# A four-stage transformer block as one software pipeline: a third hand-written order for each engine, and 18 counter increments per round in TensorE's queue

## The chip, the cores and the metric

One Trainium2 chip, one of its cores. The core has five engines that run their own instruction queues and meet only at semaphores: TensorE (PE in the profile, its weight loads PEld), VectorE (DVE), ScalarE (ACT), GpSimd (POOL) and SyncE (SP, which only starts transfers here). The metric is the device time of one execution in microseconds, the median of several runs.

## The reference

The input `x` is 128 x 64 x 128 in float32, or 64 tiles of 128 rows by 128 features; the context has the same shape. Four blocks follow each other, and the first three add their result to `x` after a layer norm without gain or bias:

```python
x = x + attention0(layernorm(x), ctx)     # 16 heads of 8, with biases, softmax over a row of 64 context positions
x = x + experts(layernorm(x))             # 8 experts 128->128->128 with relu, weights from the top 2 of a gate
x = x + attention1(layernorm(x), ctx)     # 16 heads of 8, no biases
x = x + recurrent(layernorm(x))           # the recurrence below
# recurrent, over 128 time steps of 64 rows:
f = sigmoid(xt @ wf.T + c @ uf.T + bf)
i = sigmoid(xt @ wi.T + c @ ui.T + bi)
g = tanh(xt @ wc.T + c @ uc.T + bc)
c = f * c + i * g
h = tanh(x @ wo.T + c_final @ uo.T + bo)  # needs the last c, for every tile
```

Two facts set the shape of the work. Each of the first three blocks is local to a tile (a tile is two sequences of 64). The fourth carries the state `c` through all 128 half tiles in order, and the output of every tile needs the last state.

## The kernel before, in words

Everything stays on chip: `x` and the context are read once, in 11 chunks each, and the output is written once at the end. The work is cut into rounds. In round `i` each engine does its part of every stage, for tiles of different age: the stages of the first attention work on tile `i` less a lag, those of the experts 5 tiles behind (`L1`), the second attention 8 behind (`L2`), the recurrence 13 behind (`L3`). Rounds run from 0 to 79 (`FIRST`, `LAST`). Rounds 0 to 14 fill the pipeline, in rounds 15 to 62 every stage has a tile, after that the stages run dry one by one.

Within a round each engine's operations stand in an order written out by hand, as a list of `for r in due(i, name)` loops (for TensorE lines 547 to 628, for ScalarE 824 to 903, for VectorE 1118 to 1232, for GpSimd 1365 to 1408). `LAG` says how many rounds after its tile's number an operation comes; `AHEAD` moves an operation by whole rounds in one phase of the kernel, and `due` makes up for the move where phases meet (it runs an operation twice in a round or not at all). The kernel before has two orders per engine: one for rounds 0 to 62 and one for rounds 63 to 79 (`LATE = NT + -1`). In the second, most operations are moved back by a round, so that round 63 has little in it.

TensorE's operations, with the names that the text uses and the lines of the profile: `kv` keys and values of a tile (L308, L309, L317), `turnx` transposes of the normalized rows (L331), `q` queries (L346), `S` scores (L366), `e0` to `e3` transposes of the exponentials (L381), `rt` (L392), `pv` attention times values (L411), `p` output projection (L425), `gate` (L435), `h0` and `h1` first expert layer (L446), `turnw` (L456), `y0` and `y1` second expert layer (L467), `yb` expert bias (L479), `wx0` and `wx1` the output's input share (L492, L508), `xin` the recurrence's input share (L526), `sA` and `sB` the recurrence's two half steps (L539). In float32 each matmul of the code is two passes in the queue, each a weight load and a matmul; the transposes are one. `sA`, `sB`, `pv`, `S` and half of `kv` consist of many small passes on parts of the array, the others of whole ones.

The half step `sA` needs the state `C`. After it ScalarE takes three activations (`gA`, L815 to L817) and VectorE three operations (`uA`, L1093 to L1097), which make the next `C`; then `sB`, `gB`, `uB` likewise. `xin` of the next tile waits for the `C` of `uB` (line 524).

PSUM has eight banks. One holds the recurrence; the other seven are given out in turn to the results of TensorE's operations. `USES` lists the operations in TensorE's order with the reader that frees the bank, and each operation waits for that reader. Where an operation has several waits, the last one rides on its first pass and the others are instructions of their own in TensorE's queue, two waits each.

A full round of the kernel before has 236 passes, so 472 weight loads and matmuls, and 22 waits of their own: 494 instructions (495 where a chunk of the context begins).

Of the kernel before, what the change touches and what calls it, by code (L numbers as in the profile page):

```python
# [34 lines left out]
WARM = 4  # L35

# [10 lines left out]
LAG = {"pv": 5, "sA": 2, "y0": 3, "e3": 4, "q": 2, "yb": 3, "turnx": 1, "e0": 4, "p": 5, "wx0": 10, "y1": 3,  # L47
# [7 lines left out]
OFF = (0, L1, L2, L3)  # L55
LAST_STEP = NT + L3 - 1 + LAG["sB"] - -1
FIRST, LAST = 0, NT + 16

SPAN = {"C": (0, NT), "N": (0, NT + L3), "A": (0, NT + L2), "F": (L1, NT), "Z": (L3, NT),
        "W0": (LAST_STEP - 6 - LAG["wx0"], (NW + 1) // 2), "W1": (LAST_STEP - 6 - LAG["wx1"], NW // 2)}  # L60
# [4 lines left out]
USES = [("pv", "aT", 5, "A", 1, 1), ("y0", "acc", 3, "F", 8, 5), ("e3", "ET3", 4, "A", 1, 1),  # L65
# [7 lines left out]
USES_LAST = [("y0", "acc", 3, "F", 8, 5), ("y1", "xm", 3, "F", 1, 1), ("kv", "kvc", 1, "C", 1, 1),  # L73
# [7 lines left out]


FULL, LATE = FIRST, NT + -1
AHEAD = {"y0": (0, 0, -1), "q": (0, 0, -1), "turnx": (0, 0, -1), "e0": (0, 0, -1), "p": (0, 0, -1),
# [12 lines left out]


def phase(i):
    return 0 if i < FULL else 1 if i < LATE else 2  # L100
# [13 lines left out]
def build(nc, x_d, c_d, w_d, out):  # L114
    ctx = ExitStack()
    with ctx:
# [104 lines left out]
        for i in range(FIRST, LAST):  # L221
            for name, reader, lag, chain, step, first in (USES_LAST if i >= LATE else USES):
                made = 0
                for r in due(i, "S" if name[0] == "S" else name):
                    n = r - lag - SPAN[chain][0]
                    if name == "kv" and n <= 0:
# [6 lines left out]
                place += max(made, 1)  # L233
# [49 lines left out]
        def tensor_program(e):  # L283
            def bank(i, name, done=()):
# [6 lines left out]
                return banks[bank_at[name, j]]  # L291

# [144 lines left out]
            def hidden(i, c):  # L437
# [20 lines left out]
            def experts(i, c):  # L458
# [7 lines left out]
                for n in range(4):  # L466
                    m = e.matmul(b[:, 128 * n:128 * n + 128], hT[:, t % 2, 4 * c + n, :], w2[:, 4 * c + n, :],  # L467
                                 start=True, stop=True, skip_group_check=True)
                m.then_inc(sig(f"y{c}"), 1)
# [11 lines left out]
            def out_inputs(i, u):  # L481

                g = 2 * (i - LAST_STEP + 6) + u
# [12 lines left out]
            def inputs_share(m):  # L496

                lo = TAIL[MINE[m]][1]
                if m == 0:

                    for name, reader, _, chain, step, first in USES:
# [14 lines left out]
            def cell_inputs(i):  # L516
# [30 lines left out]
            for i in range(FIRST, LATE):  # L547
                if i == FIRST + 2:
                    project_bias()
                values(i)  # L550
                step(i, 0)
                for r in due(i, "y0"):
                    experts(r, 0)
                turn_e(i, 3)
                for r in due(i, "q"):
                    query(r)
                expert_bias(i)
                for r in due(i, "turnx"):
                    turn_x(r)
                for r in due(i, "e0"):  # L560
                    turn_e(r, 0)
                for r in due(i, "p"):
                    project(r)
                out_inputs(i, 0)
                for r in due(i, "y1"):
                    experts(r, 1)
                for r in due(i, "e2"):
                    turn_e(r, 2)
                for r in due(i, "e1"):
                    turn_e(r, 1)  # L570
                for r in due(i, "gate"):
                    gate(r)
                for r in due(i, "turnw"):
                    turn_w(r)
                for r in due(i, "rt"):
                    turn_r(r)
                for r in due(i, "h0"):
# [3 lines left out]
                out_inputs(i, 1)  # L581
# [8 lines left out]
            for i in range(LATE, LAST):  # L590
                for r in due(i, "y0"):
                    experts(r, 0)
                for r in due(i, "y1"):
                    experts(r, 1)
                for r in due(i, "kv"):
                    keys_values(r)
                out_inputs(i, 0)
                for r in due(i, "sB"):
                    step(r, 1)
                for r in due(i, "turnx"):  # L600
                    turn_x(r)
                for r in due(i, "p"):
                    project(r)
                for r in due(i, "e1"):
                    turn_e(r, 1)
                for r in due(i, "turnw"):
                    turn_w(r)
                out_inputs(i, 1)
                for r in due(i, "q"):
                    query(r)  # L610
                for r in due(i, "e0"):
                    turn_e(r, 0)
                for r in due(i, "gate"):
                    gate(r)
                for r in due(i, "e2"):
                    turn_e(r, 2)
                for r in due(i, "h0"):
                    hidden(r, 0)
                turn_e(i, 3)
                for r in due(i, "S"):  # L620
                    scores(r)
                for r in due(i, "h1"):
                    hidden(r, 1)
                for r in due(i, "xin"):
                    cell_inputs(r)
                expert_bias(i)
                step(i, 0)
# [880 lines left out]
```

## Time and profile before

| | us |
|---|---|
| three timed runs | 846.52, 847.08, 849.42 (median 847.08) |
| profiled execution, span from the first to the last instruction | 848.5 |
| busy in it: PE / PEld / DVE / ACT / POOL | 822.1 / 739.4 / 769.7 / 783.1 / 686.1 |

The profiled execution was not timed separately; its span lies within the three times, 1.4 us above their median. Busy time counts how long an engine has something in hand. For TensorE it is modelled from pipelined passes, so a busy PE need not be a full one: how far apart the same operation starts in successive rounds tells more. Waits and semaphore increments are instructions of the queue, but are not counted as busy and stand in no row.

### The profile page before, as it was taken

Reading aid. Unit: us, or ns where it says so; the run is one execution under the profiler, and the core shown is the slowest. Engines: PE = TensorE matmul, PEld = TensorE weight load, DVE = VectorE, ACT = ScalarE, POOL = GpSimd, SP = SyncE. Lnnn points to the kernel's source line nnn. Section 1 sums busy time; section 2 is a strip of 40 time slices with the busy share of each in tenths; the row PEclk is TensorE's granted clock in tenths of the full one; section 3 lists DMA queues with packets and bytes.
Section 4 is the critical chain, followed back from the end, with each engine's and each line's share of the span. In section 5 each row is a group of like instructions: output and inputs, shape, how many; then the busy total and the mean of one; then the engine's idle time right before and its main releaser. Section 6 shows DMA issues by size and latency. Waiting matters only on the chain. (4 is left out here: it accounts for less than half of the span.)

```text
span 848.5 us, 41475 instructions
## 1 busy us (share of the span) xinstructions
PE 822.1 (97%) x15268; PEld 739.4 (87%) x15268; DVE 769.7 (91%) x2778; ACT 783.1 (92%) x2490; POOL 686.1 (81%) x1292
## 2 busy tenths in 40 slices
PE   7899999999999999999999999999999999999996
PEld 4688898999999999999999899999998988888784
DVE  5689999999999999999999999999999998999755
ACT  4899999999999999999999999999999999988864
POOL 4788998888888888888888888888888887877634
PEclk7899999999999999999999999999999999999999
DMA  9400000000000000000000000000000000000005
GB/s 348 166 2 3 2 3 4 3 3 4 3 4 3 3 3 3 4 3 4 3 3 3 3 4 3 3 4 3 3 3 3 4 3 3 3 4 3 3 3 199
DMA packets 6965, 17.67 MB, mean 21 GB/s; under 512 B 752, under 2 KB 2288, under 8 KB 6768
## 3 DMA queue, kind: packets, MB, share of 16 engines
q1 hardware_dynamic: 6336, 14.36, 4.4%
q8 instruction: 125, 2.05, 1.0%
q10 hardware_dynamic: 432, 0.68, 0.2%
q14 instruction: 72, 0.59, 0.2%
HBM read 10.84 MB, written 4.19 MB: 18 GB/s over the span
## 5 line engine op out<-in xcount | busy, mean ns | idle before, releaser
L976 DVE TENSOR_REDUCE mx<-ps 128x8 f32<-128x512 f32 (+1 forms) x288 | 166.8, 621 | 11.9 <-PE ps L366 11.8
L1305 POOL TENSOR_TENSOR h<-Ex 128x512 f32<-128x512 f32 (+1 forms) x144 | 166.0, 1153 | 10.7 <-ACT Ex L734 8.1
L990 DVE TENSOR_TENSOR Ex<-ps,mx 128x512 f32<-128x512 f32 (+1 forms) x288 | 167.4, 622 | 0.0
L745 ACT ACTIVATE ET<-ps 128x512 f32<-128x512 f32 (+1 forms) x288 | 155.3, 573 | 11.1 <-PE ps L381 8.9
L734 ACT ACTIVATE Ex<-Ex 128x512 f32<-128x512 f32 (+1 forms) x288 | 163.8, 596 | 0.0
L1082 DVE SCALAR_TENSOR_TENSOR acc<-ps,we,acc 128x128 f32<-128x128 f32 x448 | 150.9, 337 | 11.9 <-PE ps L467 0.5
L783 ACT ACTIVATE hT<-ps,w 128x128 f32<-128x128 f32 x512 | 149.0, 400 | 4.7 <-PE ps L446 4.6
L381 PE MATMUL ps<-w,Ex 128*128 128x128 f32 x1024 | 149.8, 275 | 1.5 <-ACT qT L722 0.7
L446 PEld LDWEIGHTS ps<-xT,w 128*128 128x128 f32 x1024 | 124.1, 191 | 24.8 <-issue 24.6
L446 PE MATMUL ps<-xT,w 128*128 128x128 f32 x1024 | 142.2, 282 | 0.0
L467 PE MATMUL ps<-w,hT 128*128 128x128 f32 x1024 | 139.5, 281 | 0.3 <-DVE Ex L990 0.3
L467 PEld LDWEIGHTS ps<-w,hT 128*128 128x128 f32 x1024 | 123.7, 192 | 5.5 <-DVE Ex L990 0.5
L381 PEld LDWEIGHTS ps<-w,Ex 128*128 128x128 f32 x1024 | 119.4, 142 | 4.3 <-ACT qT L722 1.8
L1289 POOL TENSOR_TENSOR rs<-ve,half 128x4 f32<-128x4 f32 (+3 forms) x77 | 71.6, 929 | 59.5 <-DVE ve L966 59.5
L707 ACT ACTIVATE xn<-x,mr,rs 128x128 f32<-128x128 f32 x256 | 109.7, 540 | 6.1 <-POOL mr L1291 6.1
L1309 POOL TENSOR_TENSOR h<-h 128x256 f32<-128x256 f32 (+1 forms) x144 | 97.6, 678 | 20.7 <-POOL h L1305 0.4
L366 PE MATMUL ps<-Km,qT 32*64 32x256 f32 x2048 | 75.1, 394 | 4.0 <-ACT xT L691 1.1
L539 PE MATMUL ps<-CG,w 128*32 128x64 f32 x3072 | 70.3, 222 | 3.0 <-issue 2.2
L1262 POOL TENSOR_TENSOR Km<-kT,w 128x512 f32<-128x512 f32 x64 | 66.6, 1041 | 6.0 <-ACT kT L662 5.8
L411 PE MATMUL ps<-ET,Vb 128*32 128x64 f32 x4096 | 71.2, 220 | 0.0
L1262 POOL TENSOR_TENSOR Km<-kv,w 128x512 f32<-128x512 f32 x64 | 66.7, 1042 | 0.2 <-issue 0.2
L411 PEld LDWEIGHTS ps<-ET,Vb 128*32 128x32 f32 x4096 | 65.9, 110 | 0.4
(108 smaller groups left out, 1793.7 us busy)
## 6 DMA issues: line engine op xcount, KB each, us to landing
cx<-ctx_dram SPq DMA_DIRECT2D x7, 512.0 KB, 12.3
x<-x_dram SPq DMA_DIRECT2D x7, 512.0 KB, 14.1
out_dram<-x SPq DMA_DIRECT2D x14, 256.0 KB, 2.7
w<-weights_dram SPq DMA_DIRECT2D x2, 512.0 KB, 5.8
w<-weights_dram SPq DMA_DIRECT2D x1, 576.0 KB, 8.5
out_dram<-x SPq DMA_DIRECT2D x4, 128.0 KB, 2.6
w<-weights_dram ACTq DMA_DIRECT2D x1, 328.0 KB, 5.2
w<-weights_dram ACTq DMA_DIRECT2D x1, 256.0 KB, 3.1
```

Source lines behind the costliest of these rows:

```text
L381: m = e.transpose(b[:, 128 * n:128 * n + 128], Ex[:, j % 2, r, 128 * n:128 * n + 128], ident)
L411: m = e.matmul(b[32 * r:32 * r + 32, 128 * c + 64 * n:128 * c + 64 * n + 64], Vb[:, c, j % 4, n, r, 2 * w:2 * w + 2, :].rearrange("p a c - ...
L446: m = e.matmul(b[:, 128 * n:128 * n + 128], w1[:, 4 * c + n, :], xT[:, (t + L1) % 2, 1, :], start=True, stop=True, skip_group_check=True)
L467: m = e.matmul(b[:, 128 * n:128 * n + 128], hT[:, t % 2, 4 * c + n, :], w2[:, 4 * c + n, :], start=True, stop=True, skip_group_check=True)
L734: e.activation(Er, Er, ACT.Exp, scale=SCALE).then_inc(sig(f"E{r}"), 1)
L745: e.activation(ET[:, j % 2, r, lo:hi, :, :], b[:, 256 * lo:256 * hi].rearrange("p (c w q) -> p c w q", c=hi - lo, w=2), ACT.Copy).then_inc ...
L783: m = e.activation(hT[:, t % 2, k, :], b[:, 128 * n:128 * n + 128], ACT.Relu, bias=col[:, B1 + k:B1 + k + 1])
L976: e.tensor_reduce(mx[:, j % 2, r, 4 * lo:4 * hi], b[:, 256 * lo:256 * hi].rearrange("p (j k) -> p j k", k=64), AX.X, ALU.max).then_inc(sig ...
L990: e.tensor_tensor(Ex[:, j % 2, r, 256 * lo:256 * hi].rearrange("p (j k) -> p j k", k=64), b[:, 256 * lo:256 * hi].rearrange("p (j k) -> p ...
L1082: m = e.scalar_tensor_tensor(x[:, t, :] if n == 8 else d, b[:, 128 * k:128 * k + 128], we[:, t % 2, n - 1:n], d, ALU.mult, ALU.add)
L1262: e.tensor_tensor(Km[:, j % 2, c, :, :], k.unsqueeze(1).to_broadcast([P, 4, 128]), hmask.unsqueeze(2).to_broadcast([P, 4, 128]), ALU.mult) ...
L1305: e.tensor_tensor(u, v[:, :, :, 0:32], v[:, :, :, 32:64], ALU.add).then_inc(sig("half1"), 1)
```

## The change

Three things. First, each engine has three orders: for rounds 0 to 14, 15 to 71 and 72 to 79. All three are new; `LAG`, `AHEAD` and the bank plan `USES` are rewritten to fit (one plan per phase). Second, six places of TensorE's program call `filler(1)`, which puts an instruction into the queue that computes nothing and raises a semaphore `fill` that nobody waits for: after each of the four matmuls of `h0`, `h1`, `y0`, `y1` and after two of the three of `xin`, 18 in a round, from tile 2 on. Third, the loops are written so that every operation goes through `due`. No arithmetic, no transfer and no semaphore between engines is added or taken away.

```diff
+EVEN = 2
+STARTS = (0, 15, 72)
+FIRST, LAST = STARTS[0], 80
+OUT = NT + 9
 def phase(i):
-    return 0 if i < FULL else 1 if i < LATE else 2
+    return max(sum(i >= s for s in STARTS) - 1, 0)
...
+            def filler(n):
+                for _ in range(n):
+                    e.nop(nofuse=True).then_inc(sig("fill"), 1)
...  (in hidden and experts)
                 for n in range(4):
                     m = e.matmul(b[:, 128 * n:128 * n + 128], w1[:, 4 * c + n, :], xT[:, (t + L1) % 2, 1, :],
                                  start=True, stop=True, skip_group_check=True)
+                    filler(t >= EVEN)
...  (in cell_inputs, of three)
+                    filler(t >= EVEN and n < 2)
```

TensorE's orders, in the names of above:

```
before, rounds 0-62:  pv sA y0 e3 q yb turnx e0 p wx0 y1 e2 e1 gate turnw rt h0 sB wx1 S h1 xin kv
before, rounds 63-79: y0 y1 kv wx0 sB turnx p e1 turnw wx1 q e0 gate e2 h0 e3 S h1 xin yb sA pv rt
after, rounds 0-14:   pv y0 e3 q yb turnx p e0 wx0 y1 e2 gate e1 turnw rt sA h0 wx1 S h1 xin sB kv
after, rounds 15-71:  sA pv yb y0 e3 wx0 turnx e1 p e0 wx1 y1 e2 gate q rt turnw h0 sB S h1 xin kv
after, rounds 72-79:  turnw gate h0 e1 p turnx y1 y0 wx1 e0 q kv e2 h1 e3 xin S sA pv rt wx0 sB yb
```

VectorE's in the full rounds (`mx`, `sb` maxima and differences of the scores, `c0` to `c8` the experts' sums, `st`, `ag` the layer norms' statistics):

```
before: sb1 mx2 mx3 sb2 sb3 aT sm c0 st0 c1 rc c2 xa c3 c4 c5 uA c6 gsc c7 c8 st13 st2 gtop ag uB gidx mx0 mx1 sb0
after:  st2 st13 ag uB mx1 mx0 mx2 sb1 gidx sb0 sb2 aT c0 sm mx3 c1 sb3 c2 rc c3 xa c4 uA c5 st0 c6 gsc c7 c8 gtop
```

ScalarE and GpSimd are reordered in the same way, with `gA` behind the first exponential and `gB` before the last one on ScalarE. A full round of TensorE's queue now has 494 + 18 = 512 instructions (513 in six of the full rounds, where a chunk begins).

## Rows read from the trace of the kernel before

**Rows 1.** The page's first part: span, busy time and count of each engine.

```profile
span 848.5 us, 41475 instructions
PE 822.1 (97%) x15268; PEld 739.4 (87%) x15268; DVE 769.7 (91%) x2778; ACT 783.1 (92%) x2490; POOL 686.1 (81%) x1292
```

**Rows 2.** Busy time by stretch: from:to, length, busy (instructions) by engine, PEclk, DMA.

```profile
14.90:27.00 12.10, 10.89 (x89) 6.83 (x93) 7.16 (x27) 7.38 (x25) 8.21 (x15) 0.50 1.03 408
...
38.70:117.30 78.60, 74.30 (x1141) 65.94 (x1137) 71.66 (x260) 72.65 (x235) 68.42 (x143) 1.00 0.01 3
117.30:684.80 567.50, 565.26 (x11100) 521.92 (x11096) 543.17 (x1927) 554.06 (x1741) 485.90 (x894) 1.00 0.01 3
684.80:829.90 145.10, 140.13 (x2653) 123.39 (x2644) 119.22 (x475) 123.43 (x422) 100.72 (x207) 1.00 0.01 3
```

**Rows 3.** TensorE in order of time: start, length, line, passes [idle before <-releaser].

```profile
117.33 1.08 PE L411 MATMUL ps<-ET,Vb 128*32 128x64 f32 x64
...
322.49 1.08 PE L411 MATMUL ps<-ET,Vb 128*32 128x64 f32 x64
...
323.83 1.16 PE L467 MATMUL ps<-w,hT 128*128 128x128 f32 x8
...
329.29 1.06 PE L446 MATMUL ps<-xT,w 128*128 128x128 f32 x8
...
330.75 1.12 PE L366 MATMUL ps<-Km,qT 32*64 32x256 f32 x32
...
334.46 1.08 PE L411 MATMUL ps<-ET,Vb 128*32 128x64 f32 x64
335.36 0.52 PE L539 MATMUL ps<-CG,w 128*32 128x64 f32 x24
...
684.85 1.08 PE L411 MATMUL ps<-ET,Vb 128*32 128x64 f32 x64
```

**Rows 4.** TensorE in order of time, where the half step is cut in two.

```profile
130.19 0.39 PE L539 MATMUL ps<-CG,w 128*32 128x64 f32 x10
130.99 0.42 PE L539 MATMUL ps<-CG,w 128*32 128x64 f32 x14 [0.41 <-issue]
...
467.16 0.28 PE L539 MATMUL ps<-CG,w 128*32 128x64 f32 x4
467.94 0.53 PE L539 MATMUL ps<-CG,w 128*32 128x64 f32 x20 [0.50 <-issue]
...
480.00 0.39 PE L539 MATMUL ps<-CG,w 128*32 128x64 f32 x13
480.70 0.41 PE L539 MATMUL ps<-CG,w 128*32 128x64 f32 x11 [0.31 <-issue]
```

**Rows 5.** The view of waits: who waited for what, us in total, times, longest.

```profile
PE ps L539 <- issue: 2.2, 6, 0.5
```

**Rows 6.** The DMA queues: packets, MB, share of 16 engines.

```profile
q8 instruction: 125, 2.05, 1.0%
```

**Rows 7.** The page's fifth part: the shortest weight loads of TensorE.

```profile
L411 PEld LDWEIGHTS ps<-ET,Vb 128*32 128x32 f32 x4096 | 65.9, 110 | 0.4
```

**Rows 8.** The recurrence in a full round, all engines in order of time.

```profile
331.30 0.32 ACT L817 ACTIVATE CG<-ps,w 128x64 f32<-128x64 f32 x1
...
332.14 0.23 DVE L1097 SCALAR_TENSOR_TENSOR CG<-ps,ig 128x64 f32<-128x64 f32 x1
...
332.79 0.83 PE L526 MATMUL ps<-cx,w 128*128 128x128 f32 x6
```

**Rows 9.** TensorE in order of time, at the change of orders and at the end.

```profile
698.33 0.23 PE L479 MATMUL ps<-b2s,weT 72*128 72x128 bf16 x1 [0.74 <-ACT kv L672]
...
825.71 0.54 PE L539 MATMUL ps<-CG,w 128*32 128x64 f32 x24 [0.41 <-DVE CG L1097]
...
827.84 0.91 PE L526 MATMUL ps<-cx,w 128*128 128x128 f32 x6 [0.43 <-DVE CG L1097]
```

More of the change, by code:

```diff
@@ L221, in build @@
         for i in range(FIRST, LAST):
-            for name, reader, lag, chain, step, first in (USES_LAST if i >= LATE else USES):
+            for name, reader, lag, chain, step, first in USES[phase(i)]:
                 made = 0
@@ L232, in build @@
                         made += 1
-                place += max(made, 1)
+                place += max(made, i >= 0)
         def bank_of(name, j):
@@ L499, in inputs_share @@
                 if m == 0:
-                    for name, reader, _, chain, step, first in USES:
+                    for name, reader, _, chain, step, first in USES[0]:
                         if name != "turnx":
@@ L576, in tensor_program @@
                     turn_r(r)
+                for r in due(i, "sA"):
+                    step(r, 0)
+                for r in due(i, "h0"):
+                    hidden(r, 0)
+                for r in due(i, "wx1"):
+                    out_inputs(r, 1)
+                for r in due(i, "S"):
+                    scores(r)
+                for r in due(i, "h1"):
+                    hidden(r, 1)
+                for r in due(i, "xin"):
+                    cell_inputs(r)
+                for r in due(i, "sB"):
+                    step(r, 1)
+                for r in due(i, "kv"):
+                    keys_values(r)
+            for i in range(STARTS[1], STARTS[2]):
+                for r in due(i, "sA"):
+                    step(r, 0)
+                for r in due(i, "pv"):
+                    values(r)
+                for r in due(i, "yb"):
+                    expert_bias(r)
+                for r in due(i, "y0"):
+                    experts(r, 0)
+                for r in due(i, "e3"):
+                    turn_e(r, 3)
+                for r in due(i, "wx0"):
+                    out_inputs(r, 0)
+                for r in due(i, "turnx"):
+                    turn_x(r)
+                for r in due(i, "e1"):
+                    turn_e(r, 1)
+                for r in due(i, "p"):
+                    project(r)
+                for r in due(i, "e0"):
+                    turn_e(r, 0)
+                for r in due(i, "wx1"):
+                    out_inputs(r, 1)
+                for r in due(i, "y1"):
+                    experts(r, 1)
+                for r in due(i, "e2"):
+                    turn_e(r, 2)
+                for r in due(i, "gate"):
+                    gate(r)
+                for r in due(i, "q"):
+                    query(r)
+                for r in due(i, "rt"):
+                    turn_r(r)
+                for r in due(i, "turnw"):
+                    turn_w(r)
                 for r in due(i, "h0"):
@@ L589, in tensor_program @@
                     keys_values(r)
-            for i in range(LATE, LAST):
+            for i in range(STARTS[2], LAST):
+                for r in due(i, "turnw"):
+                    turn_w(r)
+                for r in due(i, "gate"):
+                    gate(r)
+                for r in due(i, "h0"):
+                    hidden(r, 0)
+                for r in due(i, "e1"):
+                    turn_e(r, 1)
+                for r in due(i, "p"):
+                    project(r)
+                for r in due(i, "turnx"):
+                    turn_x(r)
+                for r in due(i, "y1"):
+                    experts(r, 1)
@@ new lines, in tensor_program @@
+                for r in due(i, "h1"):
+                    hidden(r, 1)
+                for r in due(i, "e3"):
+                    turn_e(r, 3)
+                for r in due(i, "xin"):
+                    cell_inputs(r)
+                for r in due(i, "S"):
+                    scores(r)
+                for r in due(i, "sA"):
+                    step(r, 0)
+                for r in due(i, "pv"):
+                    values(r)
+                for r in due(i, "rt"):
+                    turn_r(r)
@@ L598, in tensor_program @@
+                for r in due(i, "wx0"):
+                    out_inputs(r, 0)
                 for r in due(i, "sB"):
                     step(r, 1)
[L600 to L625, printed above, removed]
@@ L626, in tensor_program @@
-                expert_bias(i)
-                step(i, 0)
-                values(i)
-                for r in due(i, "rt"):
-                    turn_r(r)
+                for r in due(i, "yb"):
+                    expert_bias(r)
             for n in (5, 6):
@@ L823, in scalar_program @@
             e.activation(identb[:, :], ident, ACT.Copy).then_inc(sig("identb"), 1)
-            for i in range(FIRST, LATE):
-                if i == FIRST + 8:
+            for i in range(FIRST, STARTS[1]):
+                if i == 8:
                     e.wait_ge(sig("in_w6"), 16)
@@ new lines, in scalar_program @@
+            for i in range(STARTS[2], LAST):
+                for r in due(i, "re1"):
+                    relus(r, 1)
+                for r in due(i, "sc"):
+                    scale(r)
+                for r in due(i, "xo0"):
+                    out_inputs(r, 0)
+                for r in due(i, "gB"):
+                    gates(r, 1)
+                for r in due(i, "ET1"):
+                    turn_e(r, 1)
+                for r in due(i, "xT"):
+                    turn_x(r)
+                for r in due(i, "ex3"):
+                    exps(r, 3)
+                for r in due(i, "ex1"):
+                    exps(r, 1)
+                for r in due(i, "xo1"):
+                    out_inputs(r, 1)
+                for r in due(i, "ET0"):
+                    turn_e(r, 0)
+                for r in due(i, "re0"):
+                    relus(r, 0)
+                for r in due(i, "qc"):
+                    query(r)
+                for r in due(i, "ET2"):
+                    turn_e(r, 2)
+                for r in due(i, "wd"):
+                    widen(r)
+                for r in due(i, "ET3"):
+                    turn_e(r, 3)
+                for r in due(i, "ex0"):
+                    exps(r, 0)
+                for r in due(i, "gA"):
+                    gates(r, 0)
+                for r in due(i, "weT"):
+                    turn_w(r)
@@ L1117, in vector_program @@
             e.memset(acc[:, :, :], 0.0).then_inc(sig("zeros"), 1)
-            for i in range(FIRST, LATE):
-                if i == FIRST + 3:
+            for i in range(FIRST, STARTS[1]):
+                if i == 3:
                     e.wait_ge(sig("bvo"), 1)
@@ L1159, in vector_program @@
                     combine(r, 8)
+                for r in due(i, "gtop"):
+                    gate_top(r)
+            for i in range(STARTS[2], LAST):
+                for r in due(i, "xa"):
+                    project(r)
+                for r in due(i, "uB"):
+                    update(r, 1)
+                for r in due(i, "sm"):
+                    sums(r)
                 for r in due(i, "st13"):
                     stats_attention(r)
+                for r in due(i, "c2"):
+                    combine(r, 2)
@@ L1199, in vector_program @@
+                for r in due(i, "uA"):
+                    update(r, 0)
+                for r in due(i, "c1"):
+                    combine(r, 1)
                 for r in due(i, "c8"):
```

445 lines of the change are left out of this document (275 added, 170 removed), and 73 rows, old and new, of tables (AHEAD, LAG, USES, USES_LAST).

## The prediction, made before the changed kernel ran

> **What bounds the kernel now.** I read the page's busy times first, then the busy times by stretch, then TensorE in order of time, and last the waits and the DMA queues. TensorE is busy for 97% of the span, the others for 81 to 92% [rows 1], but a share says little where every engine is near its limit. The stretches cut the run into a fill up to 117.3 us, full rounds up to 684.8, a drain up to 829.9, and 18.6 us at the end in which the last state becomes the output [rows 2]. The full rounds are two thirds of the time. There TensorE has 565.26 us of 567.50 in hand, ScalarE 554.06, VectorE 543.17 [rows 2]: TensorE is the bound, and ScalarE is only 2.4% behind it.
>
> The reader should then take one operation and see how far apart it starts. `pv` starts at 322.49 and at 334.46, 11.97 us apart (11.975 over several such rounds) [rows 3], and in such a round no gap stands between TensorE's groups. 47 rounds lie between the `pv` of 117.33 and that of 684.85: 567.52 us, or 12.07 a round [rows 3]. At 11.975 each they would take 562.8. So 4.7 us were lost in the full rounds, though not evenly.
>
> The loss has one face. Six times the half step on L539 is cut in two, and TensorE is idle before its second part with "issue" as the reason, which means that nothing of another engine held it [rows 5]. In the second of these rows the first part starts at 467.16 with 4 passes and the rest follows at 467.94; four passes of this kind take under 0.1 us, so the cut costs some 0.7 us [rows 4]. The cuts come in pairs, in successive rounds, and the place moves: after 4 passes and then after 13 [rows 4]; the pair at 130 us moves from 10 to 19, the one at 636 us, whose rows look the same, from 1 to 10. Nine passes are 18 instructions. A round has 494 instructions, so a place that moves on by 18 per round is a place that comes every 512 instructions of the queue. Queue 8 brought TensorE's instructions in 125 packets [rows 6]; 30,536 weight loads and matmuls [rows 1] and some 1,560 waits, counted in the program, over 125 make 257 for a packet. Two packets are 512. So the cuts sit at the edge between two blocks of instructions, of 256 each. Numbering the queue's instructions, all six lie before number 197 of a block as the program counts it.
>
> Not every edge costs. Edges pass through the whole round, about one position in 27 rounds, and only those that fall into the half step behind `pv` cut. The reason must be that the block just left was short: from the scores (330.75), where the edge before it lies, to the half step (335.36) is 4.6 us for 256 instructions [rows 3], against 6 on average, and the passes there are so small that TensorE has no work in hand to cover a late block.
>
> **The change, part by part.** *The 18 increments, what they fix.* The edges are pinned. I counted the new queue, round by round, from the orders and the waits; the same count gives the old queue's 494s and places. From round 16 on the two edges of a round lie at positions 48 and 304 of 512, and drift to 42 and 298 by round 64 because of six rounds of 513. The first is where `sA` ends and `pv` begins, the second where `h0` begins. In the clean round from the end of the half step (323.83) to `h0` (329.29) are 5.46 us [rows 3]; `pv`, now behind the half step, adds 0.89 (from 322.49 to the half step behind it). So the blocks take 6.35 and 11.98 - 6.35 = 5.63 us: neither is near 4.6. In the old kernel the edges stood in the same part of the work in rounds 24, 38 and 53, and `pv` came 11.98 us apart there. The holes go: -4.7 us.
>
> *What they cost.* No row shows such an instruction. Below, zero, since they stand between whole matmuls of 0.11 us a pass, four instructions to 0.22 us, which is time in which the queue runs ahead; less than zero is excluded, as they only add. Above, if nothing covered them and each cost what the shortest weight load takes, 110 ns [rows 7], 18 x 0.11 = 1.98 us a round and 123 us over 62 tiles. I take zero: the 22 waits of a round are likewise instructions of their own, 16 of them directly before such groups, and the groups follow without idle time. The cover is gone where TensorE's queue has run empty, which in full rounds it does only at the cuts.
>
> The Trainium skill has a rule that speaks against the whole idea: the page "Runtime: NRT & Kernel Launch", section "Instruction fetch mechanics", says that the engine fetches the next block of 256 instructions by itself and that crossing a boundary is "mostly hidden". The spacing of the cuts agrees with its 256, but the six cuts are not hidden. By that rule the cuts would have another cause and would stay, and the sum would be 4.7 us higher. The page "PSUM — Partial Sum Buffer", section "Engine vs sequencer instructions", says that a nop with an increment waits only until earlier instructions are handed over, not until they complete; no run here shows it yet, and it would price the increments at nothing.
>
> *The middle order, rounds 15 to 71.* TensorE does the same passes. The kinds of neighbours that cost a longer step (whole passes to small ones and back) come as often as before, so I give the round 11.98 us again; the bounds are -0.1, if the odd gap around `yb` closes, and what a new wait would bring, below. It also replaces the old second order in rounds 63 to 71. At the change of orders before, TensorE is idle for 0.74 us in round 63 [rows 9]. Now a change comes at round 15, where all stages begin to be full, and one at 72, where little is left. I charge 1 us for round 15, by the one at 63 and a little for what follows it.
>
> *The first order, rounds 0 to 14.* Up to 27 us the DMA engines are full (share 1.03, the clock at 0.50 of its full rate) [rows 2] and no order brings the data sooner: 0. From 38.7 to 117.3 TensorE is idle for 4.3 us, ScalarE for 5.95 and VectorE for 6.9 [rows 2]. An order that fits can win at most ScalarE's 5.95, since its work stays the same, and a bad one could lose as much. I take -2, a third.
>
> *The last rounds.* From 684.8 to 829.9 TensorE is idle for 5.0 us [rows 2], part of it waits of 0.4 us for the state [rows 9], which no order removes: half steps are serial. I take -3 of a possible -5, with the other end at +3.
>
> *The rest.* The output part after 829.9 is the same, as are transfers and their order on SP: 0.
>
> Sum, on the profiled execution: 848.5 - 4.7 + 0 + 1 - 2 - 3 = 839.8. The span is 1.4 us above the median of the runs, so the time comes to 838.4 us.
>
> **The rivals.** *A: the sum holds*, 838.4, with 833 to 843 for its own range. *B: the cuts go, the ends give nothing* or lose a little: 847.1 - 4.7 + 1 = 843.4, up to 847. For it: all three engines are above 91% busy in the fill already; against it: both old orders were also used for rounds that they do not fit. *C: a new wait in every full round*, my case on the slower side. Its place is the recurrence: in a clean round ScalarE ends `gB` at 331.62, VectorE makes `C` by 332.37, and `xin` starts at 332.79 [rows 8], with 0.4 us to spare. VectorE now does `uB` behind both statistics and the aggregation, and ScalarE has some 0.28 us free in a round. If the chain comes 0.25 us too late in 50 rounds, 12.5 us are added: 851. It decides from 0.17 us a round, where it eats the 8.7 us gained. Against it: `uB` stood behind the same three before, and `S` and `h1` (2 us) still lie between `sB` and `xin`. *D: the edges are pinned where they hurt.* My count could be off by some instructions at the start. If each of 50 rounds had a cut of 0.7 us: 838.4 + 35 = 873. The nearest bad place is 85 instructions behind the first edge in the old order, so the miscount would have to be large. *E: the increments aren't covered*: 838.4 + 123 = 961 at the upper bound. *F: the cuts are something else and stay*, the page's rule above: as a mechanism, the half step would be cut once the queue has been drained by `pv`, whatever the block. 838.4 + 4.7 = 843.1. Against it, the step of exactly 9 passes in all three pairs.
>
> **How the numbers follow.** A 0.57, B 0.16, C 0.13, D 0.05, E 0.03, F 0.06. I call a change of under 0.3%, or 2.5 us (844.5 to 849.6), no change. Faster: A, F and half of B, 0.71. Same: the rest of B and the mild part of C, 0.11. Slower: most of C, D and E, 0.18. The predicted time is A's, 838.4. The range takes in A, B, F and C up to its price: 832 to 851.
>
> **What would show it.** Cuts on L539 with "issue" gone, and `pv` at 11.98 us in every round from 16 to 64: the pinned edges are right. A cut in the same place of each round: D. More than 1.0 us from the start of `h0` or `y1` to what follows its 8 passes: E. A wait of `xin` for `C` or of TensorE for ScalarE in each round: C. If the first `pv` of round 15 does not come before 117 us and the drain after round 65 is not shorter, the orders for the ends gave nothing. The prediction is wrong if the full round is not 11.98 us.

## The result, and the profile after

The changed kernel takes 841.29 us (841.05 to 841.61, four runs), the kernel before took 847.14 on the same chip: ratio 0.9923, 95% interval 0.9904 to 0.9942. The forecast was 838.4, with 832 to 851 as its range. The profiled execution lasted 839.2 us against 848.5, so on the profiles the gain is 9.3 us, in the timed runs 5.9. That difference has a cause. In every run of which both are known, the time is 1.75 to 2.1 us above the span of the same execution (841.05 and 839.2 for this profile). So the profile of before, at 848.5, is of an execution of some 850.3 us, 3 us slower than the median; where most of that lay is told below.

The page of the kernel after, its first part, beside [rows 1]:

```profile
span 839.2 us, 42592 instructions
PE 820.6 (98%) x15268; PEld 743.5 (89%) x15268; DVE 775.3 (92%) x2778; ACT 775.4 (92%) x2490; POOL 682.5 (81%) x1292
```

TensorE makes the same 15,268 passes; the page counts 1,117 instructions more, of which 1,116 are the increments (18 for 62 tiles). Queue 8 brings 129 packets, where [rows 6] had 125. The busy times by stretch (from:to, length, busy with instructions, PEclk, DMA), cut at the first pass of round 7, 15, 62, 72 and 79, beside [rows 2]:

```profile
34.90:111.70 76.80, 74.72 (x1145) 65.96 (x1141) 71.48 (x259) 72.01 (x234) 68.09 (x143) 1.00 0.01 3
111.70:680.60 568.90, 568.90 (x11103) 527.02 (x11094) 547.17 (x1926) 547.78 (x1741) 483.69 (x896) 1.00 0.01 3
680.60:784.50 103.90, 102.61 (x1953) 93.78 (x1944) 98.53 (x380) 95.06 (x322) 81.75 (x169) 1.00 0.01 3
784.50:821.90 37.40, 35.33 (x728) 30.94 (x725) 22.26 (x102) 27.78 (x100) 17.20 (x34) 1.00 0.01 3
```

The same view of the kernel before, for the stretches from round 62 and from round 72, which it enters at 684.85 and 785.41:

```profile
684.80:785.40 100.60, 99.30 (x1879) 88.27 (x1870) 92.03 (x352) 91.28 (x304) 80.96 (x168) 1.00 0.01 3
785.40:829.20 43.80, 40.13 (x770) 34.42 (x769) 27.19 (x123) 31.53 (x116) 19.75 (x40) 1.00 0.01 3
```

Look at the second line of after. TensorE is busy for all of 568.90 us, without a hole, and yet the 47 rounds take 1.4 us *longer* than the 567.50 of before with its six cuts [rows 2]. The cuts are gone, and every round has become longer: 12.096 us where none is disturbed, against 11.977. TensorE in order of time shows it (start, length, line, passes):

```profile
305.83 1.10 PE L423 MATMUL ps<-ET,Vb 128*32 128x64 f32 x64
...
311.40 0.29 PE L447 MATMUL ps<-w,xT 128*128 128x8 f32 x2
311.55 0.69 PE L358 MATMUL ps<-xT,w 128*128 128x128 f32 x4
312.07 0.38 PE L404 MATMUL ps<-w,rd 128*128 128x128 f32 x2
312.29 0.22 PE L469 MATMUL ps<-identb,wep 128*72 128x128 bf16 x1
312.35 1.11 PE L458 MATMUL ps<-xT,w 128*128 128x128 f32 x8
313.39 0.54 PE L554 MATMUL ps<-CG,w 128*32 128x64 f32 x24
...
317.93 1.10 PE L423 MATMUL ps<-ET,Vb 128*32 128x64 f32 x64
```

`pv` (now L423) starts at 305.83 and at 317.93, 12.10 us apart; in [rows 3] it was 11.97. The places that grew are here: `q` (L358) takes 0.52 us until the next group starts, behind the gate's 8 columns (L447), where the old order gave it 0.446; and `h0` (L458) takes 1.04 us behind the single pass of `turnw` (L469), where it took 0.986 behind `rt`. These two make 0.08 + 0.05 us, and `rt` and `turnw` between them give 0.01 back: 0.12 us a round. The same groups of before, for comparison:

```profile
325.26 0.61 PE L346 MATMUL ps<-xT,w 128*128 128x128 f32 x4
325.71 0.22 PE L479 MATMUL ps<-b2s,weT 72*128 72x128 bf16 x1
...
329.00 0.23 PE L456 MATMUL ps<-identb,wep 128*72 128x128 bf16 x1
329.06 0.39 PE L392 MATMUL ps<-w,rd 128*128 128x128 f32 x2
329.29 1.06 PE L446 MATMUL ps<-xT,w 128*128 128x128 f32 x8
330.28 0.54 PE L539 MATMUL ps<-CG,w 128*32 128x64 f32 x24
```

`h1`, `y1` and `xin`, which carry increments too, start as far from what follows them as before (0.995, 0.894 and 0.670 us).

### The profile page after: what moved, and what is told of

It reads as the page before. It is cut to its first block, busy times and chain, and to the rows that moved or that the text cites. A ratio compares the mean times of both kernels' runs of the same rounds, so it can differ in the third digit from the quotient of the medians.

```text
span 839.2 us, 42592 instructions
## 1 busy us (share of the span) xinstructions
PE 820.6 (98%) x15268; PEld 743.5 (89%) x15268; DVE 775.3 (92%) x2778; ACT 775.4 (92%) x2490; POOL 682.5 (81%) x1292
## 4 chain that ended last, share of the span: by engine, by line
PE 90%; DVE 4%; ACT 3%; issue 2%; POOL 1%; DVEq 0%; POOLq 0%; ACTq 0%
PE ps L458 15%; PE ps L480 13%; PE ps L393 13%; PE ps L378 8%; PE ps L423 7%; PE ps L554 6%; PE ps L540 5%; PE ps L329 4%; PE ps L358 4%; PE ps L437 3%; PE ps L343 3%; PE ps L320 2%; PE ps L404 2%; PE ps L321 2%; PE ps L493 1%
## 5 line engine op out<-in xcount | busy, mean ns | idle before, releaser
L1120 DVE TENSOR_TENSOR Ex<-ps,mx 128x512 f32<-128x512 f32 (+1 forms) x288 | 170.8, 617 | 0.1
L819 ACT ACTIVATE ET<-ps 128x512 f32<-128x512 f32 (+1 forms) x288 | 166.0, 584 | 3.2 <-PE ps L393 2.9
L393 PE MATMUL ps<-w,Ex 128*128 128x128 f32 x1024 | 158.8, 275 | 0.1
L1212 DVE SCALAR_TENSOR_TENSOR acc<-ps,we,acc 128x128 f32<-128x128 f32 x448 | 147.9, 330 | 1.3 <-issue 0.2
L458 PEld LDWEIGHTS ps<-xT,w 128*128 128x128 f32 x1024 | 124.2, 191 | 24.6 <-issue 24.6
L458 PE MATMUL ps<-xT,w 128*128 128x128 f32 x1024 | 144.9, 284 | 0.0
L857 ACT ACTIVATE hT<-ps,w 128x128 f32<-128x128 f32 x512 | 140.1, 398 | 3.1 <-PE ps L458 2.8
L393 PEld LDWEIGHTS ps<-w,Ex 128*128 128x128 f32 x1024 | 121.4, 143 | 1.7 <-ACT qT L796 0.5
L423 PE MATMUL ps<-ET,Vb 128*32 128x64 f32 x4096 | 71.9, 220 | 0.0
L554 PE MATMUL ps<-CG,w 128*32 128x64 f32 x3072 | 68.2, 221 | 0.8 <-DVE CG L1227 0.8
L889 ACT ACTIVATE ps<-ps,w 128x64 f32<-128x64 f32 x128 | 36.8, 288 | 34.2 <-PE ps L554 33.8
```

The lines of the kernel that those rows point to most:

```text
L393: m = e.transpose(b[:, 128 * n:128 * n + 128], Ex[:, j % 2, r, 128 * n:128 * n + 128], ident)
L819: e.activation(ET[:, j % 2, r, lo:hi, :, :], b[:, 256 * lo:256 * hi].rearrange("p (c w q) -> p c w q", c=hi - lo, w=2), ACT.Copy).then_inc ...
L857: m = e.activation(hT[:, t % 2, k, :], b[:, 128 * n:128 * n + 128], ACT.Relu, bias=col[:, B1 + k:B1 + k + 1])
L1120: e.tensor_tensor(Ex[:, j % 2, r, 256 * lo:256 * hi].rearrange("p (j k) -> p j k", k=64), b[:, 256 * lo:256 * hi].rearrange("p (j k) -> p ...
L1212: m = e.scalar_tensor_tensor(x[:, t, :] if n == 8 else d, b[:, 128 * k:128 * k + 128], we[:, t % 2, n - 1:n], d, ALU.mult, ALU.add)
```

## The experiments

**One part at a time.** Four kernels ran beside each other: the changed kernel without the increments, the old orders with them, the increments begun later so that the edges move, and the new middle order with two pairs of operations put back.

```diff
 e1:                 for _ in range(n):
-                    e.nop(nofuse=True).then_inc(sig("fill"), 1)
+                    pass
```

> The changed kernel with its three orders, but filler() puts nothing into TensorE's queue, so that a full round has 494 instructions again. Theory (the 0.12 us by which the full round grew comes from the new order, and the cuts come from block edges that drift through the round): a round without a cut stays at 12.10 us, and cuts of 0.4 to 0.9 us come back in pairs of rounds, some 4 to 5 us in all, each pair 18 instructions apart: 845 to 846.5 us. Rival (the increments cost 0.12 us a round): the uncut round falls to 11.98 us, which over 50 rounds gives back 6 us, and with the cuts the time is 839 to 841 us. Rival (new orders alone avoid cuts): 841 us and no cuts.

Measured: 841.97 us, ratio to before 0.9938 (0.9921 to 0.9954), as the kernel after within the error. The undisturbed round is 12.086 us against 12.096 with increments, so they cost at most 0.01 us of it and not the 0.12. The theory was right on the round and missed the time (845 to 846.5 us), and the rival held by which the new orders alone avoid cuts: they hardly return. Four rounds are 0.05 to 0.13 us longer than a clean one, two others 0.03, no more. With the new orders the increments have little left to do.

```diff
 e2 (before, with the filler calls of the change):
+EVEN = 2
+                    filler(t >= EVEN)      # in hidden and experts
+                    filler(t >= EVEN and n < 2)   # in cell_inputs
```

> The kernel before with its own orders and only the 18 increments per round added; by the count of the queue its edges then lie 47 instructions into pv and at the start of h0 in all full rounds. Theory: full rounds of 11.98 us and no cut, so the 4.7 us of the cuts are saved and nothing else: 842.4 us, with 841.5 to 843.5. Rival (the increments cost 0.12 us a round): rounds of 12.10 us, 847 to 848 us. Rival (block edges are not the cause of the cuts): the cuts stay in six rounds and the time is 847 us.

Measured: 845.24 us, ratio 0.9974 (0.9959 to 0.999), a gain of 2.2 us (0.8 to 3.5) in the timed runs, less than the 4.7 that I had expected. No group of small passes is cut any more, and the stretch from round 15 to 62 takes 563.58 us where before took 567.52:

```profile
115.40:678.90 563.50, 563.50 (x11100) 520.96 (x11092) 542.12 (x1927) 553.91 (x1741) 485.75 (x894) 1.00 0.01 3
```

So in the old orders 18 increments bring 3.9 us in these rounds of the profile, and leave rounds of 11.98 us. The six cuts of before had lengthened their rounds by 4.0 us (0.70, 0.70, 0.86, 0.60, 0.65 and 0.49); the other 0.6 of the 4.7 lay in six rounds that were 0.06 to 0.17 longer without a listed cut, and e2 has ten such rounds of 0.03 to 0.09. The trace records each increment as a semaphore event of 51 ns, about 0.15 us apart between whole passes, and about 1 us ahead of the passes in hand. By the Trainium skill, page "PSUM — Partial Sum Buffer", section "Engine vs sequencer instructions", such an increment waits for no pass to complete; the trace agrees, with that 1 us.

```diff
-EVEN = 2
+EVEN = 8      # e3: the changed kernel
```

> The changed kernel with EVEN = 8 instead of 2: the increments begin six tiles later, 108 instructions fewer, so that the edges lie about 103 instructions into pv and 38 into the scores in every full round, where in the kernel before the edges of the cut rounds lay (counted from the start of the small passes). Theory: a cut of 0.4 to 0.9 us near the end of pv in each of some 49 rounds, full rounds of 12.5 to 13.0 us, 861 to 885 us. Rival (the cuts need something else than the place of the edge, such as the old order of pv and sA): no cuts, 841 us.

Measured: 841.66 us, ratio 0.9927 (0.9911 to 0.9944), no cut, where the theory had 861 to 885 us. My theory, that the edges only had to lie in a bad place, failed in the new order.

```diff
 e4 (TensorE, rounds 15 to 71, and its bank plan):
-gate, q, rt, turnw, h0
+q, gate, turnw, rt, h0
```

> The changed kernel; in rounds 15 to 71 TensorE's order is q, gate, turnw, rt, h0 instead of gate, q, rt, turnw, h0 (bank plan to fit), which are the neighbours that these operations had before. In the trace q after gate takes 0.08 us longer than q after e3, and h0 after turnw 0.05 us longer than h0 after rt. Theory (the step after a pass of 8 columns or of bf16 costs this): full round of 11.97 to 11.98 us, 50 to 57 rounds x 0.12 = 6 to 7 us less, 834.5 to 836 us. Rival (the bound is a chain through another engine): the idle time moves and the round stays at 12.10 us, 841 us.

Measured: 835.71 us, ratio 0.9858 (0.9842 to 0.9875): 5.6 us better than the changed kernel (5.5 by the two ratios). TensorE in order of time, the same stretch of a round:

```profile
322.50 0.61 PE L358 MATMUL ps<-xT,w 128*128 128x128 f32 x4
322.94 0.29 PE L447 MATMUL ps<-w,xT 128*128 128x8 f32 x2
323.08 0.23 PE L469 MATMUL ps<-identb,wep 128*72 128x128 bf16 x1
323.15 0.39 PE L404 MATMUL ps<-w,rd 128*128 128x128 f32 x2
323.37 1.06 PE L458 MATMUL ps<-xT,w 128*128 128x128 f32 x8
```

`q` takes 0.44 us until the next group, `h0` 0.98 (until 312.38 from 311.40 in the round before), the round 11.97. Eight of the 47 rounds are 0.15 to 0.17 us longer, 1.3 us in all; the extra lies between `sA` and `pv`, at the pinned edge, as in the three rounds of 12.25 us of the changed kernel. From round 15 to 62 it takes 564.04 us, 4.9 less than after:

```profile
112.40:676.50 564.10, 564.08 (x11104) 521.55 (x11100) 547.41 (x1926) 549.02 (x1741) 485.31 (x896) 1.00 0.01 3
```

TensorE is busy for all of this stretch too. Its busy time can't tell the two orders apart, the distance between starts does.

**Does the place of an edge matter at all?** e3 had said no for the new order. In the old one the question was open.

```diff
-EVEN = 2
+EVEN = 8      # e5: otherwise e2
```

> The kernel before, with its own orders, and 18 increments per round that start with round 8 of the hidden steps instead of round 2. Every full round then has 512 instructions, and by my count of the queue its two edges lie 19 to 20 instructions into the half step sA (L539 of before) and 37 to 38 into the scores S, in each of some 48 rounds. In the kernel before, six of the rounds whose edge lay near there had a cut of 0.42 to 0.72 us in sA.
> Theory (in the old order the place of the edge decides): a cut of 0.4 to 0.9 us in most of the 48 rounds, rounds of 12.4 to 12.9 us instead of 11.98, in all 865 to 885 us.
> Rival (a cut needs more than the place: a fetch of code that comes late for another reason): no cut or a few, rounds of 11.98, about 845 us, as with the increments from round 2 on (845.2).

Measured: 865.59 us, ratio 1.0198 (1.0181 to 1.0215). The theory held: 34 of the 47 rounds from 15 to 61 are longer than 12.12 us, by 20.0 us together. The time is at the low end of the 865 to 885 expected. The waits of this kernel (who waited for what, us in total, times, longest), where [rows 5] had 2.2 us:

```profile
PEld ps L548 <- issue: 17.1, 39, 0.8
PE ps L548 <- issue: 10.8, 28, 0.6
```

And two of its cuts in order of time, both after 11 passes, where the count had put the edge after 10:

```profile
263.79 0.39 PE L548 MATMUL ps<-CG,w 128*32 128x64 f32 x11
264.45 0.42 PE L548 MATMUL ps<-CG,w 128*32 128x64 f32 x13 [0.27 <-issue]
...
276.33 0.39 PE L548 MATMUL ps<-CG,w 128*32 128x64 f32 x11
277.25 0.42 PE L548 MATMUL ps<-CG,w 128*32 128x64 f32 x13 [0.53 <-issue]
```

```diff
 e6: e5, and TensorE, rounds 0 to 62:
-                values(i)
-                step(i, 0)
+                step(i, 0)
+                values(i)
```

> The kernel of e5 (old orders, edges pinned 19 to 20 into sA and 37 to 38 into S), with one thing changed: on TensorE the half step sA comes before the values pv in rounds 0 to 62, as in none of the other orders of before. The pair of passes of sA that were cut then stands next to others and the queue's own wait for the gates ends elsewhere.
> Theory (what made the kernel after nearly immune is which pass waits ahead of the edge: pv behind sA instead of sA behind pv): no cut or a few, rounds of 11.98 to 12.0, 843 to 846 us, even if e5 has cuts in most rounds.
> Rival (the immunity lies in the rest of the new order, or the place alone decides): cuts as in e5, the same time as e5 within 3 us. If e5 has no cuts, this run says only what the swap costs by itself: -0.5 to +0.5 us over the whole time.

Measured: 862.38 us, ratio 1.0165 (1.0147 to 1.0183). 22 rounds are longer than a clean one by 0.3 us or more, 16.0 us together, and the cut has moved with the edge, into `pv`:

```profile
433.64 0.94 PE L417 MATMUL ps<-ET,Vb 128*32 128x64 f32 x50
435.14 0.42 PE L417 MATMUL ps<-ET,Vb 128*32 128x64 f32 x14 [0.56 <-issue]
```

So it is not the half step that is cut but whatever lies at the edge, and the order of these two alone is not what protects the changed kernel. e6 has its edges where e3 has them (some 104 instructions into `pv`, 38 into `S`) and the same operations from `S` to `pv`; e3 has no cut.

The traces let one check the count itself. Number TensorE's records in order of time, two for each pass and one for each wait or increment, from the first in the profile. Before, e5, e6, e7 and e11 then have 60 pauses of more than 0.35 us between two weight loads of one group in rounds 15 to 62 (6, 28, 21, 4 and 1), and in all 60 the first load behind the pause has number 193 or 194 of its 256. The number of such edges in each trace is also that of queue 8's packets, 125 without increments and 129 with them. So the cuts lie at the edges, whatever passes stand there.

**What is late in a cut.** The trace has the start of each packet of queue 8. In e3, without cuts, the packet behind the edge in `S` starts 0.6 to 2.3 us after the weight load at that edge (median 1.4); in the cut rounds of before, e5 and e6 it starts 2.3 to 3.1 us after it. The next edge comes 4.4 to 4.6 us after the first, and TensorE goes on 2.2 to 2.9 us after the packet's start, in all 57 cuts of these three kernels that stop the weight loads for more than 0.35 us from one to the next. Nowhere in the full rounds of the twelve traces is a block entered less than 2.2 us after its packet has started. Late packet and early edge together make the cut.

Part of why the packet is late can be read from the increments, which TensorE's queue records as it comes to them. Those of one group are 0.15 us apart. In e6, behind the edge in `S`, one step is 0.3 us instead, and the packet starts 0.2 to 1.2 us after it, mostly 0.7. Between 125 and 680 us, in 19 of the 21 uncut rounds the long step ends 0.4 to 1.0 us after the edge, in 19 of the 20 cut rounds 1.8 to 2.0 us after it. So the lateness shows in TensorE's own queue before the packet starts; no packet of the other instruction queue goes with the cuts regularly. That this step is the request for the packet is my reading and not shown, and what puts it at the one or the other moment, and why seldom late in the new orders, stays open. The Trainium skill, page "Runtime: NRT & Kernel Launch", section "Instruction fetch mechanics", calls the crossing of a block "mostly hidden": e2, e3 and the changed kernel agree with it, 34 rounds of e5 don't.

**Are the increments still worth anything?**

```diff
 e7: e4, and
-                    e.nop(nofuse=True).then_inc(sig("fill"), 1)
+                    pass
```

> The kernel of e4 (the changed kernel with TensorE's middle order mended: q, gate, turnw, rt, h0) without the 18 increments, so 494 instructions a round and edges that drift through the round.
> Theory (the new orders alone avoid the cuts, as in e1, where three rounds were 0.04 to 0.13 us longer than a clean one; the increments are now worth 0.7 us at most): rounds of 11.97 us, 835.5 to 836.5 us against 835.7 with increments.
> Rival (with q and gate in the mended places the cuts come back when the edges drift, as in the kernel before): six or so cuts of 0.4 to 0.8 us, 838 to 841 us.

Measured: 836.54 us, ratio 0.9848 (0.9832 to 0.9865). The time can't be told from e4's. On the profile round 15 to 62 takes 565.09 us, 1.05 more than e4: four rounds are 0.4 to 0.6 us longer, each with a pause at an edge in `pv`. So a drifting edge can still be cut in the mended order, where e1 had no such round. The increments are worth about 1 us on this profile, and nothing that the timed runs show.

```diff
 e8 (the changed kernel, TensorE, rounds 15 to 71):
-gate, q, rt, turnw, h0
+gate, q, turnw, rt, h0
```

> The kernel after, with turnw and rt of TensorE's middle order swapped back (gate, q, turnw, rt, h0): h0 stands behind rt as in the kernel before, q still behind the 8 columns of the gate.
> Theory (two exposures make the longer round: q behind gate 0.08 us, h0 behind turnw 0.05 us, and they add up): the clean round is 12.04 to 12.05 us, between 11.97 of the mended order and 12.095 of the changed kernel, and the time about 838.5 us (837.5 to 839.5).
> Rival 1 (q alone makes all of it): 12.10 us, 841 to 842 us. Rival 2 (h0 alone, or the two only together): 11.97 us, about 835.7 us.

Measured: 839.26 us, ratio 0.9889 (0.9872 to 0.9905). The clean round is 12.05 us. The two exposures add up: 11.97, 12.05, 12.095.

**What protects the new order, and what the first order brings.**

```diff
-EVEN = 2
+EVEN = 8      # e11: otherwise e4
```

> The kernel of e4 (middle order mended: q, gate, turnw, rt, h0) with the increments from hidden step 8 instead of 2, so that the edges lie some 103 instructions into pv and 38 into S, as in e3, where there was no cut in any round. In e5 and e6 edges at the same places gave cuts in about 37 and 25 of 48 rounds, so what protects the changed kernel is not the place and not the order of sA and pv alone.
> Theory (the protection lies in the new order as a whole, in the stretch between pv and S or in the other engines' orders, and not in q standing behind the gate): no cut or a few, rounds of 11.97, 835.5 to 837.5 us.
> Rival (q behind the gate and rt ahead of turnw is what protects; e7 with the mended order had one cut of 0.3 us and more in pv, e1 had none): cuts of 0.2 to 0.9 us in half of the rounds, 845 to 855 us.

Measured: 835.32 us, ratio 0.9864 (0.9848 to 0.9881), one cut (at 150 us, in `pv`) and all other rounds from 16 to 61 at 11.97 or 11.98. The theory held: `q` behind the gate and `rt` ahead of `turnw` are not the protection. The remaining candidates are the rest of the stretch from `pv` to `S` and the orders of the other engines; they were not tried one by one.

```diff
-STARTS = (0, 15, 72)
+STARTS = (0, 11, 72)      # e12: otherwise e4
```

> The kernel of e4 with the middle order from round 11 on instead of from round 15, on every engine; the first order is left for rounds 0 to 10. From the first pass of round 11 to that of round 15 the kernel before took 43.80 us, the changed one 42.68 and e4 42.73.
> Theory (what the fill gained between rounds 7 and 15, 1.85 us in ten profiles alike, comes from an order that fits the filling rounds): the middle order, made for full rounds, gives it back in part, so this stretch takes 43.2 to 44.5 us, and the time is 836.2 to 837.5 us against 835.7.
> Rival (any of the new orders does as well as the first; the gain came from the lags or from the early rounds): 42.5 to 43.0 us, 835.5 to 836 us.

Measured: 838.2 us, ratio 0.9899 (0.9882 to 0.9915), 2.5 us more than e4 and 2.9 more than e11, which ran on the same chip; 836.2 to 837.5 us had been expected. The stretch from round 11 to 15, e4 first, then e12:

```profile
69.70:112.40 42.70, 41.84 (x662) 37.66 (x656) 41.76 (x137) 40.25 (x121) 38.56 (x74) 1.00 0.01 3
```

```profile
71.00:115.70 44.70, 41.11 (x665) 37.59 (x657) 42.21 (x138) 40.45 (x122) 40.01 (x76) 1.00 0.01 3
```

TensorE is idle for 3.6 us instead of 0.9. The middle order doesn't fit the rounds that fill; the loss is just above what I had given it (44.72 us from start to start, against 43.2 to 44.5).

The best kernels are e4, e7 and e11, at ratios of 0.9858, 0.9848 and 0.9864, which beat both originals and can't be told from each other.

## Why the forecast was right, step by step

The time fell into the range and the direction was right, but that it came this close is luck: errors of opposite sign met in the sum. The prediction's own last line, that it is wrong if the full round is not 11.98 us, went against it: the round is 12.096. Round starts of the two profiles give each term.

*The cuts, -4.7.* Right in the main. The six are gone; they were 4.0 of it. The mechanism was right for the old orders: e2 removes them by pinning alone, e5 brings them into 34 rounds by pinning badly. It is not needed for the new ones (e1, e3). The reason given, that the block just left was short, is half of it: e3 passes the same stretch in 4.4 us and is not cut, and the packet must also be late.

*The increments, 0.* Right: e2 keeps 11.98 us, e1 gains 0.01 a round. Rival E is out, though the sign that was to show it, more than 1.0 us from the start of `h0` to what follows, came: `h0` takes 1.04 us with and without increments (e1), so the sign could not tell E from a new neighbour.

*The middle order, 0.* This is the step that failed. "The kinds of neighbours that cost a longer step come as often as before" looked at whole passes beside small ones, and not at whole passes behind a pass of 8 columns or a single bf16 pass. The round is 12.096 us, 47 x 0.12 = +5.6 us, and three rounds of 12.25 add 0.45. e4 and e8 show both places and that they add up. Why a group takes longer behind a short pass no run shows.

*The hand-over at round 15, +1.* It costs nothing: rounds 15 and 16 take 12.09 us each.

*The first order.* For rounds 7 to 14 I took -2; it is 78.62 to 76.76 us, -1.9, and the profiles of e2, e5 and e6 (78.5 to 78.7) and of e1, e3, e4, e7 and e8 (76.7 to 76.9) repeat it. e12 bears out for rounds 11 to 14 that the order matters: they take 43.80 us in the old order, 42.68 to 42.74 in the new first one and 44.72 in the middle one. Ahead of round 7 I took 0, "the DMA engines are full"; the profile says -3.8 (38.71 to 34.90). Most of that is a slow execution of before. e2, e5 and e6 have the same instructions as before up to there and reach round 7 at 36.66, 36.46 and 35.23; the seven other kernels with the new first order, at 35.0 to 37.0. What differs is when the clock is low. These are busy times by stretch, whose third number from the right is the granted clock; first the kernel before:

```profile
20.00:24.00 4.00, 3.38 (x20) 2.20 (x27) 2.07 (x10) 3.82 (x15) 2.81 (x5) 0.50 1.04 412
24.00:28.00 4.00, 4.00 (x68) 2.79 (x68) 2.74 (x8) 1.65 (x6) 1.99 (x5) 0.50 1.03 408
```

Then e6, whose queues are the same up to this time:

```profile
20.00:24.00 4.00, 3.09 (x52) 1.98 (x54) 1.88 (x10) 3.34 (x13) 2.81 (x7) 1.00 1.03 408
24.00:28.00 4.00, 3.15 (x58) 2.25 (x58) 3.64 (x15) 3.82 (x15) 3.02 (x6) 1.00 1.03 406
```

With DMA just as full, one ran at 1.2 GHz and was busy for all 4.00 us, the other at 2.4 and had time to spare. So in that execution of before TensorE at its lower clock had become the limit at the end of the loading, and the DMA share of 1.03 in [rows 2] hid it. Both sets of kernels show either level between 10 and 28 us, at different moments. The starts of round 7 follow the moment at which the clock rises and then stays up until the output: in the eight kernels with the new first order it is 20.5, 20.8, 21.1, 21.4, 25.4, 26.5, 26.8 and 27.3 us, and round 7 starts at 34.90, 35.04, 35.12, 35.48, 35.62, 35.96, 36.34 and 36.95, in the same order. In the old one it is 18.6, 24.0, 25.5 and 29.1, and 35.23, 36.66, 36.46 and 38.71. No run sets the clock by itself, so this is a regularity of twelve profiles and not an experiment.

*The last rounds, -3.* The size was short: from round 62 to the end it is 163.70 to 158.65 us, -5.05, and all the kernels with the old last order (163.7 to 164.2) and the new (158.0 to 159.0) repeat it. The stretches above show where: up to round 72 the new kernel takes 3.3 us more and makes 74 passes more, then the stretch to round 79 takes 6.4 us less, with TensorE idle for 2.1 us instead of 3.7, and round 79 up to the output another 2.0 less. The output part is the same, 14.98 and 14.99 us from the first pass of its 512-column group. Which part of the new last order does it was not tried.

On the profiles: -3.8 - 1.9 + 1.4 - 5.05 = -9.3 us. With the averages of the four old and eight new fills up to round 7 (36.8 and 35.7 us) in place of one pair, it is -6.6, and the timed 5.9 (4.9 to 8.1) agrees.

*From span to time, -1.4.* This went the wrong way. The time lies some 1.8 us above the span of its own execution, in every run. The predicted span of 839.8 us would be timed at 841.6, and it was 841.3; the 848.5 that the sum starts from was 3.2 us above what fits the median, most of it by that slow fill.

The other rivals: B, D and F are out, F by the count of the edges (D's price was real all the same: e5 paid 20 us against the 35 of the estimate, since 13 of 47 rounds had no cut and the others one of 0.6 us). C asked for a longer round from a wait for the state; the longer round came, at 0.12 us below the 0.17 where it would have decided, and from the order of TensorE's own neighbours, as e4 and e8 show, not from a wait for the state.

## What to carry to other kernels

Where an engine is busy without a hole, compare the distance between starts of each operation in both orders, by its neighbour: here a group of whole float32 passes behind a very short pass cost 0.05 to 0.08 us more, and with the two groups the other way round next to nothing. Instruction block edges are worth pinning only once a cut is seen, and then far from the stretch where 256 instructions pass in 4.5 us: the same 18 increments gained 2 us in one place and lost 17 in another. One profile of a fill says little: take its rounds from several executions before you price what an order does there, and set a profile's span beside the time of the same execution before you start a sum from it.

## What the runs showed of the hardware

An increment in TensorE's queue is recorded as 51 ns; 1,116 of them cost at most 0.01 us a round of 18 (12.096 against 12.086 us), and they are recorded about 1 us ahead of the passes. The queue's instructions come in blocks of 256, one packet of queue 8 each. A packet takes 0.9 to 1.6 us, and TensorE enters a block at the earliest 2.2 us after the packet's start; where it gets to the edge sooner it stops, and goes on 2.2 to 2.9 us after that start. And executions whose instructions are the same up to then run at either clock level between 10 and 28 us, and start round 7 at 35.2 to 38.7 us.
